# A graph network's node pipeline: bias and the second norm's h added to the convolution in its PSUM bank, x2 added from there, and no SBUF tile for x2 + h

## The chip, the core and the metric

The kernel runs on one core of a Trainium2 chip. The metric is the time of one execution on the device in microseconds, the median of several runs. The engines are named as in the profile: PE is TensorE (PEld its weight loads), DVE is VectorE, ACT is ScalarE, POOL is GpSimd, SP is SyncE.

## The reference

Four residual graph layers run over 100,000 nodes with 64 features and 25,000 edges. Most nodes are the end of no edge. For such a node a layer needs nothing but its own row:

```python
h = jnp.maximum(_layernorm(x, axis=-1), 0.0)
x = x + _L1_gnn_ref(h, src, dst, L1_gnn_fc_w, L1_gnn_fc_b)      # own row: x + h
h = jnp.maximum(_layernorm(x, axis=-1), 0.0)
x = x + _L2_gnn_ref(h, edge_index, L2_gnn_W1, L2_gnn_b1, L2_gnn_W2, L2_gnn_b2)
h = jnp.maximum(_layernorm(x, axis=-1), 0.0)
x = x + _L3_gnn_ref(h, edge_index, L3_gnn_W1, L3_gnn_b1, L3_gnn_W2, L3_gnn_b2)
```

The third layer (L2 in the names) gives `relu(h W1 + b1) W2 + b2 + h` for such a node. The row that goes into the last norm is therefore `x3 = x2 + h2 + conv + b2`, where x2 is the row before the layer, h2 its norm's output and conv the product of the second convolution. The change is in this sum.

## The kernel before

The first 560 us sort and prepare the edges. Then the main phase does two jobs at once, on the same engines, in one hand-written order:

- **Edges.** Six stages A to F, of 25 groups each. A group is 512 columns: its source rows are gathered (POOL, `mn_ring`, stages B to F), transposed, summed by a scan along the edges (`mn_total`, L1581), multiplied (`mn_scaled`, L1597), put through a weight product (L1933) and transposed back. Between two stages all rows must be in DRAM before POOL may gather them. Stage A gathers nothing; POOL meanwhile looks up 168 index tiles (`found`), which `late()` needs at the end of stage A (L1686).
- **Nodes.** 123 units of 1,024 nodes (25 of them, the "local" ones, are edge rows in stage A's order), each in a tile of 128 by 512. A unit passes through a pipeline of eight ticks; at tick t the units t to t - 7 are each at another step. The lists `TICKS_OF` say which ticks run in which group: about one in each group of A, C, E and F, two in three groups of B and D.

The steps of a tick that the change and the prediction touch, for the unit u = t - 3 where nothing else is said:

- PE, `first`, `second`, `third`: `conv1(2)` (L1206, bank 5), then further products, the edge group's `product` (L1933, it waits for `mn_scaled`), `variance(3)` (L1201), `conv2(2)` (L1211, bank 5), the transpose of x_in of unit t - 1 (bank 0), `conv2(3)` (L1211, bank 1). Then `center(3)` (L1197) reads x3 into bank 3; it waits for x3, and for `normalise(3)` of the unit before, which empties bank 3.
- ACT, `rest`: copies bank 0 to x2 of unit t - 1 (L1378); squares bank 3 (L1326); then, for units whose first norm is computed here, `row_deviation` (L1335, L1338), which stands behind those squares in ACT's order.
- DVE, `tail`: `normalise(2)` for unit t - 2 (h2, L1407), `node_res` = x2 + h2 for the same unit (L1425), x3 of unit t - 3 (L1431), `normalise(3)` for unit t - 4 (h3, L1407), and for unit t - 5 the pair y (L1442, in bank 1) and x4 (L1447). Then `h1` (L1452), which waits for ACT's `row_deviation`, and after it the edge group's scan.

Each engine takes its instructions strictly in this order; semaphores alone tie the engines together. Bank 5 holds conv1, then conv2 of one unit; PE may write the next unit's conv1 into it when x3 has been read out of it.

Of the kernel before, what the change touches and what calls it, by code (L numbers as in the profile page):

```python
# [11 lines left out]
ACT = mybir.ActivationFunctionType  # L12
# [1093 lines left out]
class Nodes:  # L1106
# [6 lines left out]
    def __init__(self, K, ctx):  # L1113
        def sb(name, r, shape=W):
            return ctx.enter_context(K["nc"].sbuf_tensor(f"node_{name}", [P, r, shape], F32))

        self.x_in, self.x2, self.res, self.x3 = sb("x_in", 3), sb("x2", 2), sb("res", 2), sb("x3", 3)
        self.h1, self.cent = sb("h1", 1), sb("cent", 1)
        self.h = {2: sb("h2", 2), 3: sb("h3", 2)}
        self.act = {2: sb("act2", 1), 3: sb("act3", 1)}  # L1120
        self.y, self.x4, self.rows = sb("y", 1), sb("x4", 2), sb("rows", 4)
        self.square, self.std = sb("square", 3), sb("std", 2)
        self.mean, self.var, self.lnv, self.rstd = (sb(a, 1, 8) for a in ("mean", "var", "lnv", "rstd"))
        self.s = sems(K["nc"], ctx, "node", "loaded:3 turned x2 res x3 y x4 outT out_rows stored:4 centered:n "
                      "squared:n var:n std:n rstd:n h:n conv1:n act:n conv2:n local_t:4 local_rows:4 mean1 cent1 x2_rows")
# [54 lines left out]
def node_tensor(K, nd, pe):  # L1180
    s, n, C, bank = nd.s, UNITS, K["C"], K["bank"]
# [96 lines left out]
    def third(t):  # L1278
        if 0 <= t - 3 < n:
            center(3, nd.x3[:, (t - 3) % 3, :], s["x3"], t - 3)  # L1280
        if local(t - 3):
            pe.wait_ge(s["x2"], t)
            turn(nd.act[2][:, 0, :], s["local_t"][2])
        if 0 <= t - 1 < n:
            center(2, nd.x2[:, (t - 1) % 2, :], s["x2"], t - 1)
        if local(t - 5):
            if local(t - 3):
                pe.wait_ge(s["local_rows"][2], t - 2)
            else:
                pe.wait_ge(s["x2"], t)  # L1290
            pe.wait_ge(s["act"][3], t - 4)
            turn(nd.act[3][:, 0, :], s["local_t"][3])
# [3 lines left out]
def node_scalar(K, nd, act):  # L1296
    s, n, C, bank = nd.s, UNITS, K["C"], K["bank"]

    def local(u):
        return 0 <= u < LOCALS  # L1300

    def log_var(i, u):
        act.wait_ge(s["var"][i], u + 1)
        need(act, s["h"][i], u)
        act.activation(nd.std[:, i - 2, :], bank[4][:, :], ACT.Ln, bias=C["eps"][:, 0:1]) \  # L1305
            .then_inc(s["std"][i], 1)

    def deviation(i, u):
        act.wait_ge(s["std"][i], u + 1)
        act.activation(nd.std[:, i - 2, :], nd.std[:, i - 2, :], ACT.Exp, scale=-0.5).then_inc(s["rstd"][i], 1)  # L1310

    def relu(i, u):
        act.wait_ge(s["conv1"][i], u + 1)
        if local(u - 1):
            act.wait_ge(s["local_t"][i], u)
        if u > 0 and i == 2:
            act.wait_ge(s["conv2"][2], u)
        elif u > LOCALS:
            act.wait_ge(s["conv2"][3], u - LOCALS)
        act.activation(nd.act[i][:, 0, :], bank[5 if i == 2 else 1][:, :], ACT.Relu, bias=C["bias"][:, 2 * i - 4:2 * i - 3]) \  # L1320
            .then_inc(s["act"][i], 1)

    def squares(i, u):
        act.wait_ge(s["centered"][i], u + 1)
        need(act, s["var"][i], u)
        act.activation(nd.square[:, i - 1, :], bank[i][:, :], ACT.Square).then_inc(s["squared"][i], 1)  # L1326

    def row_squares(u):
        act.wait_ge(s["cent1"], norms_until(u) + 1)
        act.activation(nd.square[:, 0, :], nd.cent[:, 0, :], ACT.Square).then_inc(s["squared"][1], 1)  # L1330

    def row_deviation(u):
        i = norms_until(u)
        act.wait_ge(s["var"][1], i + 1)
        act.activation(nd.lnv[:, 0, :], nd.var[:, 0, :], ACT.Ln, bias=C["eps"][:, 0:1], scale=1.0 / F) \  # L1335
            .then_inc(s["std"][1], 1)
        act.wait_ge(s["std"][1], i + 1)
        act.activation(nd.rstd[:, 0, :], nd.lnv[:, 0, :], ACT.Exp, scale=-0.5).then_inc(s["rstd"][1], 1)  # L1338

    def local_copy(kind, u):  # L1340
        act.wait_ge(s["local_t"][kind], u + 1)
        need(act, s["stored"][kind], u * 16)
        act.activation(nd.rows[:, kind, :], bank[0][:, :], ACT.Copy).then_inc(s["local_rows"][kind], 1)

    def begin(t):
        if 0 <= t - 3 < n:
            relu(2, t - 3)
        if 0 <= t - 2 < n:
            log_var(2, t - 2)

    def rest(t, between=None):
        if local(t - 3):
            local_copy(0, t - 3)
        if 0 <= t - 2 < n:
            deviation(2, t - 2)
        if LOCALS <= t - 6 < n:
            i = t - 6 - LOCALS
            act.wait_ge(s["outT"], i + 1)
            act.wait_ge(s["stored"][i % 4], 16 * (LOCALS + i // 4))
            act.activation(nd.rows[:, i % 4, :], bank[0][:, :], ACT.Copy).then_inc(s["out_rows"], 1)  # L1360
        if between:
            between()
        if 0 <= t - 5 < n:
            relu(3, t - 5)
        if 0 <= t - 4 < n:
            log_var(3, t - 4)
        if local(t - 5):
            local_copy(1, t - 5)
        if 0 <= t - 4 < n:
            deviation(3, t - 4)  # L1370
        if own_norm(t):
            row_squares(t)
        if 0 <= t - 1 < n:
            u = t - 1
            act.wait_ge(s["turned"], u + 1)
            need(act, s["centered"][2], u - 1)
            need(act, s["res"], u - 1)
            act.activation(nd.x2[:, u % 2, :], bank[0][:, :], ACT.Copy).then_inc(s["x2"], 1)  # L1378
        if 0 <= t - 3 < n:
            squares(3, t - 3)  # L1380
        if own_norm(t):
            row_deviation(t)
        if local(t - 3):
            local_copy(2, t - 3)
        if 0 <= t - 1 < n:
            squares(2, t - 1)
        if local(t - 5):
            local_copy(3, t - 5)
    return begin, rest


def node_vector(K, nd, v):
# [25 lines left out]

    def tail(t):
        if 0 <= t - 2 < n:  # L1420
            u = t - 2
            h = normalise(2, u)
            v.wait_ge(s["h"][2], u + 1)
            v.wait_ge(s["x2"], u + 1)
            v.tensor_tensor(nd.res[:, u % 2, :], nd.x2[:, u % 2, :], h, ALU.add).then_inc(s["res"], 1)  # L1425
        if 0 <= t - 3 < n:
            u = t - 3
            v.wait_ge(s["conv2"][2], u + 1)
            v.wait_ge(s["res"], u + 1)
            need(v, s["centered"][3], u - 2)  # L1430
            v.scalar_tensor_tensor(nd.x3[:, u % 3, :], bank[5][:, :], C["bias"][:, 1:2], nd.res[:, u % 2, :],  # L1431
                                   ALU.add, ALU.add).then_inc(s["x3"], 1)
        if 0 <= t - 4 < n:
            normalise(3, t - 4)
        if own_norm(t):
            v.wait_ge(s["squared"][1], norms_until(t) + 1)
            v.tensor_reduce(nd.var[:, 0, :], rows3(nd.square[:, 0, :]), AX.X, ALU.add).then_inc(s["var"][1], 1)
        if LOCALS <= t - 5 < n:
            u, i = t - 5, t - 5 - LOCALS
            v.wait_ge(s["conv2"][3], i + 1)  # L1440
            v.wait_ge(s["h"][3], u + 1)
            v.scalar_tensor_tensor(bank[1][:, :], bank[1][:, :], C["bias"][:, 3:4], nd.h[3][:, u % 2, :],  # L1442
                                   ALU.add, ALU.add).then_inc(s["y"], 1)
            v.wait_ge(s["y"], i + 1)
            v.wait_ge(s["x3"], u + 1)
            need(v, s["outT"], i - 1)
            v.scalar_tensor_tensor(nd.x4[:, u % 2, :], bank[1][:, :], 0.0, nd.x3[:, u % 3, :],  # L1447
                                   ALU.max, ALU.add).then_inc(s["x4"], 1)
        if own_norm(t):
            i = norms_until(t)  # L1450
            v.wait_ge(s["rstd"][1], i + 1)
            v.scalar_tensor_tensor(rows3(nd.h1[:, 0, :]), rows3(nd.cent[:, 0, :]), 0.0, wide(nd.rstd),  # L1452
                                   ALU.max, ALU.mult).then_inc(s["h"][1], 1)
            v.wait_ge(s["h"][1], i + 1)
            v.tensor_tensor(nd.x_in[:, t % 3, :], nd.x_in[:, t % 3, :], nd.h1[:, 0, :], ALU.add) \
                .then_inc(s["x2_rows"], 1)
# [628 lines left out]
```

## Time and profile before

| | |
|---|---|
| median of 3 runs | 2442.53 us (2442.11 to 2446.15) |
| span of the profiled execution | 2443.7 us |
| DVE, PE, POOL, ACT busy | 1845.2, 1785.7, 1781.6, 1377.4 us |
| stages A to F | A about 580 to 810 us, B to 1104, C to 1370, D to 1654, E to 1920, F to 2180, then POOL alone scatters the edge rows |

The profiled execution's own time is not given apart from its span, which lies 1.2 us above the median of the runs. A busy share over the whole span mixes the stages: what a change is worth is read from one tick of each stage.

### The profile page before, as it was taken

What the parts mean: (1) busy time and instruction counts of PE and PEld (TensorE: products, weight loads), DVE (VectorE), ACT (ScalarE), POOL (GpSimd) and SP (SyncE); (2) the same over time, 40 slices, a digit from 0 to 9 for tenths busy, and PEclk for the clock granted to TensorE, in tenths of its full rate; (3) what the DMA queues carried; (4) which work ended last, traced back from release to release, by engine and by line L of the source; (5) the groups of instructions that cost most, each with busy time, mean ns of one, the idle gap of its engine ahead of it and who ended that gap; (6) DMA issues with size and microseconds to landing.
All of it is one profiled execution on the core that took longest, in us unless ns stands there. A gap on an engine that the chain in (4) does not pass through costs nothing.

```text
span 2443.7 us, 26381 instructions
## 1 busy us (share of the span) xinstructions
PE 1785.7 (73%) x6414; PEld 872.1 (36%) x6414; DVE 1845.2 (76%) x3016; ACT 1377.4 (56%) x3086; POOL 1781.6 (73%) x1776
## 2 busy tenths in 40 slices
PE   3888888874998588878999878868999788860000
PEld 1333333322444244334444334434444344430000
DVE  6999998746888488986999688886999799960000
ACT  2766676632887365546888655546888666620000
POOL 6777777776777777736777577756777577777776
PEclk9999999986999799978999888988999899975555
DMA  3344443224776354434444356654444455440000
GB/s 71 90 124 129 127 123 97 71 75 132 233 240 216 115 182 128 133 115 107 129 131 130 102 167 188 184 170 115 128 130 129 112 139 136 129 133 22 23 21 20
DMA packets 223229, 302.24 MB, mean 124 GB/s; under 512 B 78896, under 2 KB 85165, under 8 KB 222952
## 3 DMA queue, kind: packets, MB, share of 16 engines
q1 hardware_dynamic: 166632, 249.64, 31.3%
q0 software_dynamic: 56448, 50.92, 11.6%
q8 instruction: 56, 0.92, 0.2%
q14 instruction: 93, 0.76, 0.1%
HBM read 156.13 MB, written 144.91 MB: 123 GB/s over the span
## 4 chain that ended last, share of the span: by engine, by line
DVE 23%; POOL 21%; issue 14%; PE 10%; ACT 6%; DMA 1%; DVEq 0%; POOLq 0%; SPq 0%; ACTq 0%
POOL mn_ring L529 13%; POOL out_dram L1889 8%; DVE node_h L1407 5%; PE bank L1197 5%; DVE mn_total L1581 4%; DVE node_x L1431 2%; DVE node_h L1452 1%; DVE mn_ring L1566 1%; ACT node_square L1326 1%; DVE node_mean L1414 1%; DVE mn_scaled L1597 1%; ACT node_std L1310 1%; PE bank L1206 1%; PE bank L1201 1%; PE bank L1191 1%
## 5 line engine op out<-in xcount | busy, mean ns | idle before, releaser
L529 POOL DMA_INDIRECT mn_ring<-slot_rows,addr_i x980 | 976.8, 997 | 390.4 <-issue 295.5
L1197 PE MATMUL bank<-node_x,center 128*128 128x512 f32 x492 | 250.8, 624 | 97.0 <-DVE node_h L1407 92.7
L1326 ACT ACTIVATE node_square<-bank 128x512 f32<-128x512 f32 x246 | 145.9, 593 | 222.6 <-PE bank L1197 222.6
L1201 PE MATMUL bank<-node_square,mean 128*128 128x512 f32 x492 | 265.5, 622 | 3.4 <-ACT node_std L1305 2.7
L1206 PE MATMUL bank<-node_h,wconv 128*128 128x512 f32 x492 | 266.1, 624 | 0.3 <-DVE mn_sums L1719 0.3
L529 POOL DMA_INDIRECT found<-node_table,look_i x196 | 209.7, 1070 | 74.9 <-issue 62.8
L529 POOL DMA_INDIRECT xin<-in_x_dram,src_i x192 | 195.2, 1017 | 64.3 <-issue 57.6
L529 POOL DMA_INDIRECT xin<-in_x_dram,dst_i x192 | 196.5, 1023 | 58.5 <-issue 58.5
L1889 POOL DMA_INDIRECT out_dram<-keep,scat_i x196 | 193.1, 985 | 62.5 <-issue 62.5
L1211 PE MATMUL bank<-node_act,wconv 128*128 128x512 f32 x442 | 230.9, 605 | 1.9 <-ACT node_act L1320 1.9
L1320 ACT ACTIVATE node_act<-bank,bias 128x512 f32<-128x512 f32 x246 | 170.5, 693 | 86.0 <-PE bank L1206 86.0
L1407 DVE SCALAR_TENSOR_TENSOR node_h<-bank,node_std 128x512 f32<-128x512 f32 x246 | 168.6, 686 | 54.0 <-ACT node_std L1310 52.2
L1305 ACT ACTIVATE node_std<-bank,eps 128x512 f32<-128x512 f32 x246 | 172.2, 700 | 23.1 <-PE bank L1201 22.6
L1581 DVE TENSOR_TENSOR_SCAN mn_total<-same,mn_total,bank 128x512 f32<-128x512 uint8 x120 | 150.2, 1251 | 25.6 <-PE bank L1918 25.4
L719 PE MATMUL bank<-fr_s_lo,fr_s_hi 128*128 128x392 f16 x392 | 138.5, 353 | 28.2 <-ACT fr_d_h L800 18.8
L1197 PEld LDWEIGHTS bank<-node_x,center 128*128 128x128 f32 x492 | 83.2, 194 | 211.6 <-DVE node_x L1431 152.2
L1310 ACT ACTIVATE node_std<-node_std 128x512 f32<-128x512 f32 x246 | 154.8, 629 | 5.3
L1201 PEld LDWEIGHTS bank<-node_square,mean 128*128 128x128 f32 x492 | 95.9, 199 | 136.3 <-issue 121.4
L800 ACT ACTIVATE fr_d_h<-fr_d_far,w 128x128 f16<-128x128 f16 x392 | 135.9, 394 | 6.4
L721 PE MATMUL bank<-fr_d_lo,fr_d_h 128*128 128x392 f16 x392 | 137.3, 350 | 0.0
L723 PE MATMUL bank<-fr_d_lo,fr_d_h 128*128 128x392 f16 x392 | 136.7, 349 | 0.0
L1933 PE MATMUL bank<-mn_scaled,wconv 128*128 128x512 f32 (+1 forms) x200 | 113.6, 652 | 28.9 <-DVE mn_scaled L1597 28.9
(337 smaller groups left out, 3807.0 us busy)
## 6 DMA issues: line engine op xcount, KB each, us to landing
out_dram<-node_rows SPq DMA_DIRECT2D x98, 256.0 KB, 3.4
mn_rin<-res SPq DMA_DIRECT2D x96, 256.0 KB, 3.6
slot_rows<-node_rows SPq DMA_DIRECT2D x96, 256.0 KB, 2.1
slot_rows<-keep SPq DMA_DIRECT2D x96, 256.0 KB, 2.3
mn_fcol<-f_rows SPq DMA_DIRECT2D x192, 128.0 KB
res<-mn_x SPq DMA_DIRECT2D x72, 256.0 KB, 3.0
node_x_in<-in_x_dram SPq DMA_DIRECT2D x64, 256.0 KB, 3.0
mn_ring<-slot_rows,addr_i POOLq DMA_INDIRECT x980
```

Source lines behind the costliest of these rows:

```text
L529: return eng.indirect_dma_start(out=dest, out_offset=None, in_=table, in_offset=bass.IndirectOffsetOnAxis(ap=index, axis=0))
L1197: pe.matmul(bank[i][:, :], C["center"][:, :], src, start=True, stop=True).then_inc(s["centered"][i], 1)
L1201: pe.matmul(bank[4][:, :], C["mean"][:, :], nd.square[:, i - 1, :], start=True, stop=True) \
L1206: pe.matmul(bank[5 if i == 2 else 1][:, :], C["wconv"][:, 2 * i - 4, :], nd.h[i][:, u % 2, :], start=True, stop=True) \
L1211: pe.matmul(bank[5 if i == 2 else 1][:, :], C["wconv"][:, 2 * i - 3, :], nd.act[i][:, 0, :], start=True, stop=True) \
L1305: act.activation(nd.std[:, i - 2, :], bank[4][:, :], ACT.Ln, bias=C["eps"][:, 0:1]) \
L1310: act.activation(nd.std[:, i - 2, :], nd.std[:, i - 2, :], ACT.Exp, scale=-0.5).then_inc(s["rstd"][i], 1)
L1320: act.activation(nd.act[i][:, 0, :], bank[5 if i == 2 else 1][:, :], ACT.Relu, bias=C["bias"][:, 2 * i - 4:2 * i - 3]) \
L1326: act.activation(nd.square[:, i - 1, :], bank[i][:, :], ACT.Square).then_inc(s["squared"][i], 1)
L1407: v.scalar_tensor_tensor(h, bank[i][:, :], 0.0, nd.std[:, i - 2, :], ALU.max, ALU.mult).then_inc(s["h"][i], 1)
L1581: v.tensor_tensor_scan(total[:, i % 2, 0:w], of_group(C["same"], g), source, 0.0 if g == 0 else total[:, 1 - i % 2, W - 1:W], ALU.mult, AL ...
L1889: gp.indirect_dma_start(out=K["out"], out_offset=bass.IndirectOffsetOnAxis(ap=C["scat"][:, t:t + 1], axis=0), in_=keep[:, t * F:t * F + F] ...
```

## The change

The sum x2 + h2 in SBUF is not computed. DVE adds bias and h2 of unit t - 3 to bank 5 in place, and then x2 from there to x3. h2 and x2 are thus read one tick later than before; x2 gets a third buffer for it, h2 keeps two. The semaphore `res` now counts the addition in the bank.

```diff
-        self.x_in, self.x2, self.res, self.x3 = sb("x_in", 3), sb("x2", 2), sb("res", 2), sb("x3", 3)
+        self.x_in, self.x2, self.x3 = sb("x_in", 3), sb("x2", 3), sb("x3", 3)
...
-            center(2, nd.x2[:, (t - 1) % 2, :], s["x2"], t - 1)
+            center(2, nd.x2[:, (t - 1) % 3, :], s["x2"], t - 1)
...
             need(act, s["centered"][2], u - 1)
-            need(act, s["res"], u - 1)
-            act.activation(nd.x2[:, u % 2, :], bank[0][:, :], ACT.Copy).then_inc(s["x2"], 1)
+            need(act, s["x3"], u - 2)
+            act.activation(nd.x2[:, u % 3, :], bank[0][:, :], ACT.Copy).then_inc(s["x2"], 1)
...
         if 0 <= t - 2 < n:
-            u = t - 2
-            h = normalise(2, u)
-            v.wait_ge(s["h"][2], u + 1)
-            v.wait_ge(s["x2"], u + 1)
-            v.tensor_tensor(nd.res[:, u % 2, :], nd.x2[:, u % 2, :], h, ALU.add).then_inc(s["res"], 1)
+            normalise(2, t - 2)
         if 0 <= t - 3 < n:
             u = t - 3
             v.wait_ge(s["conv2"][2], u + 1)
+            v.wait_ge(s["h"][2], u + 1)
+            v.scalar_tensor_tensor(bank[5][:, :], bank[5][:, :], C["bias"][:, 1:2], nd.h[2][:, u % 2, :],
+                                   ALU.add, ALU.add).then_inc(s["res"], 1)
             v.wait_ge(s["res"], u + 1)
+            v.wait_ge(s["x2"], u + 1)
             need(v, s["centered"][3], u - 2)
-            v.scalar_tensor_tensor(nd.x3[:, u % 3, :], bank[5][:, :], C["bias"][:, 1:2], nd.res[:, u % 2, :],
-                                   ALU.add, ALU.add).then_inc(s["x3"], 1)
+            v.tensor_tensor(nd.x3[:, u % 3, :], bank[5][:, :], nd.x2[:, u % 3, :], ALU.add).then_inc(s["x3"], 1)
```

What stands in DVE's order, in one tick of stage C, before. The names behind "waits" are those of the semaphores' numbers, some of them given to an earlier phase's name: `fr_h1T` counts conv2(2), `fr_squared` h2, `fr_xd_in0` x2, `fr_xd_in1` res, `ix_stored` center(3).

```order
1807 L1407 SCALAR_TENSOR_TENSOR node_h2<-bank2,node_std 128x512 [waits fr_rstd,fr_edges1]
1808 L1425 TENSOR_TENSOR node_res<-node_x2,node_h2 128x512 [waits fr_xd_in0,fr_squared]
1809 L1431 SCALAR_TENSOR_TENSOR node_x3<-bank5,bias,node_res 128x512 [waits ix_stored,fr_xd_in1,fr_h1T]
1810 L1407 SCALAR_TENSOR_TENSOR node_h3<-bank3,node_std 128x512 [waits fr_factor,fr_mean]
1811 L1437 TENSOR_REDUCE node_var<-node_square 128x8 [waits ix_spread]
```

And the same place in the changed kernel:

```order
1806 L1407 SCALAR_TENSOR_TENSOR node_h2<-bank2,node_std 128x512 [waits fr_rstd,fr_edges1]
1807 L1426 SCALAR_TENSOR_TENSOR bank5<-bank5,bias,node_h2 128x512 [waits fr_squared,fr_h1T]
1808 L1431 TENSOR_TENSOR node_x3<-bank5,node_x2 128x512 [waits ix_stored,fr_xd_in0,fr_xd_in1]
1809 L1407 SCALAR_TENSOR_TENSOR node_h3<-bank3,node_std 128x512 [waits fr_factor,fr_mean]
1810 L1436 TENSOR_REDUCE node_var<-node_square 128x8 [waits ix_spread]
```

The number of instructions is the same. The wait for conv2(2) stood before the second instruction behind h2, and now stands before the first. PE's order and ACT's order are unchanged.

## Rows read from the trace of the kernel before

**Rows 1.** The page: span, busy times, chain that ended last.

```profile
span 2443.7 us, 26381 instructions
...
PE 1785.7 (73%) x6414; PEld 872.1 (36%) x6414; DVE 1845.2 (76%) x3016; ACT 1377.4 (56%) x3086; POOL 1781.6 (73%) x1776
...
DVE 23%; POOL 21%; issue 14%; PE 10%; ACT 6%; DMA 1%; DVEq 0%; POOLq 0%; SPq 0%; ACTq 0%
```

**Rows 2.** Windows of stages C and F: length, busy times, PEclk, DMA share, GB/s.

```profile
1145.00:1350.00 205.00, 195.68 (x687) 97.88 (x685) 194.14 (x282) 178.66 (x443) 155.91 (x162) 1.00 0.49 129
...
1948.00:2120.00 172.00, 145.14 (x501) 71.93 (x502) 163.15 (x239) 111.10 (x209) 130.16 (x132) 1.00 0.50 137
```

**Rows 3.** Windows of x3 (L1431) alone, first to last start: length, busy.

```profile
1145.30:1349.25 203.95, 14.91 (x21) 1.00 0.49 129
1694.74:1899.25 204.51, 14.92 (x21) 1.00 0.48 129
622.28:779.79 157.51, 11.91 (x17) 1.00 0.75 240
```

**Rows 4.** Chain of waits, stage C: start, length, what.

```profile
1177.52 1.11 PE bank L1197 x2
...
1178.65 0.60 ACT node_square L1326
...
1179.47 0.22 ACT node_rstd L1338
```

**Rows 5.** Timeline of DVE, one tick of stage C: start, length, instruction.

```profile
1172.17 0.69 DVE L1597 TENSOR_TENSOR mn_scaled<-mn_total,mn_fcol 128x512 f32<-128x512 f32 x1
...
1174.70 0.68 DVE L1407 SCALAR_TENSOR_TENSOR node_h<-bank,node_std 128x512 f32<-128x512 f32 x1
1175.42 0.69 DVE L1425 TENSOR_TENSOR node_res<-node_x,node_h 128x512 f32<-128x512 f32 x1
1176.03 0.74 DVE L1431 SCALAR_TENSOR_TENSOR node_x<-bank,bias,node_res 128x512 f32<-128x512 f32 x1
1176.69 0.68 DVE L1407 SCALAR_TENSOR_TENSOR node_h<-bank,node_std 128x512 f32<-128x512 f32 x1
...
1177.88 0.75 DVE L1442 SCALAR_TENSOR_TENSOR bank<-bank,bias,node_h 128x512 f32<-128x512 f32 x1
1178.67 0.69 DVE L1447 SCALAR_TENSOR_TENSOR node_x<-bank,node_x 128x512 f32<-128x512 f32 x1
1179.71 0.69 DVE L1452 SCALAR_TENSOR_TENSOR node_h<-node_cent,node_rstd 128x512 f32<-128x512 f32 x1 [0.35 <-ACT node_rstd L1338]
```

**Rows 6.** Timeline of PE, the same tick of stage C.

```profile
1173.02 1.02 PE L1933 MATMUL bank<-mn_scaled,wconv 128*128 128x512 f32 x2
...
1174.73 1.02 PE L1211 MATMUL bank<-node_act,wconv 128*128 128x512 f32 x2
...
1177.52 1.96 PE L1197 MATMUL bank<-node_x,center 128*128 128x512 f32 x4 [0.47 <-DVE node_h L1407]
```

**Rows 7.** Timelines of DVE and PE, one tick of stage A.

```profile
642.79 0.69 DVE L1407 SCALAR_TENSOR_TENSOR node_h<-bank,node_std 128x512 f32<-128x512 f32 x1
```

```profile
643.63 1.10 PE L1197 MATMUL bank<-node_x,center 128*128 128x512 f32 x2 [0.25 <-DVE node_h L1407]
...
650.71 1.02 PE L1211 MATMUL bank<-node_act,wconv 128*128 128x512 f32 x2
```

**Rows 8.** Timeline of all engines, one tick of stage F.

```profile
1966.62 0.68 DVE L1641 TENSOR_TENSOR mn_part<-bank,mn_aux 128x512 f32<-128x512 f32 x1
...
1968.58 1.02 PE L1211 MATMUL bank<-node_act,wconv 128*128 128x512 f32 x2
...
1969.87 0.68 DVE L1407 SCALAR_TENSOR_TENSOR node_h<-bank,node_std 128x512 f32<-128x512 f32 x1
```

**Rows 9.** Waits over the span: who for whom, total us, times, longest.

```profile
POOL mn_ring L529 <- DMA slot_rows<-keep: 90.0, 4, 36.3
...
DVE mn_val L1686 <- DMA found<-node_table,look_i: 7.1, 2, 6.3
DVE node_x L1431 <- PE bank L1211: 5.1, 12, 1.2
```

## The prediction

> **What bounds the kernel now.** I read the page first. DVE is busy 76% of the span, PE and POOL 73% each, and the chain that ended last is shared by DVE (23%) and POOL (21%) [rows 1]. No engine bounds the whole, so I went on to single ticks, and of those to the three starts that the change touches: h2, conv2(2) and x3.
>
> In steady stage C, 20 ticks take 203.95 us from the first x3 to the last, 10.20 us a tick [rows 3]. The chain of waits in one of them runs from the h3 behind x3 to `center(3)` (1177.52), to ACT's squares of it (1178.65), to `node_rstd` (1179.47) and to h1 on DVE [rows 4]. DVE has been idle 0.35 us when h1 starts at 1179.71 [rows 5]. The rest of the loop is DVE's own order from h1 over the scan to the next h3. `center(3)` waited 0.47 us, and for h3, not for x3 [rows 6]. So in this stage whatever delays h3 delays `center(3)`, the squares, `node_rstd`, h1, the scan and the whole next tick. The 0.35 us is no cushion for h3: h1 starts at a fixed distance behind it (1176.69 to 1179.71, 3.02 us), through PE and ACT.
>
> POOL gathers beside this. At the four stage ends from B to F it waited 90.0 us in total, up to 36.3, for the rows of the stage before to be stored [rows 9]. A longer C or E thus moves the next stage's start by its whole length.
>
> **The change part by part.** It takes out `node_res` (0.69 us) and x3 with the bias (0.74), and puts in an addition in the bank and an addition of x2. The nearest rows for the new pair are y and x4, which do the same in bank 1: 0.75 and 0.69 [rows 5]. In busy time that is 1.43 against 1.44, nothing. What counts is start to start, and which start waits.
>
> Before, from h2: 0.72 to `node_res`, which waits for h2; 0.61 to x3, which waits for nothing of its own tick on DVE; 0.66 to h3 [rows 5]. That is 1.99. After, the first addition needs no result of this tick, so 0.61 (as from `node_res` to x3); then 0.79 to the addition of x2, which needs the first (as from y to x4, 1177.88 to 1178.67); then 0.61 to h3 (as behind `node_res`). That is 2.01: 0.02 us more. Wherever conv2(2) is early, the change costs about nothing. The one wait on h2 that goes is paid back by the one between the new pair.
>
> But conv2(2) is not early in stage C. It starts at 1174.73 and takes 1.02 [rows 6], so it ends at 1175.75. Before, it was first needed for x3 at 1176.03, which hid it. Now it is needed 0.61 behind h2, at 1175.31. With 0.04 for the semaphore (ACT started its squares 0.02 behind `center(3)`'s end, 1178.63 to 1178.65 [rows 4], and I take twice that) the first addition starts at 1175.79, the second at 1176.58, h3 at 1177.19 instead of 1176.69. **That is 0.50 us per tick.** Nothing gives it back. conv2(2) stands on PE two products behind the product of the edges (1173.02), which waits for `mn_scaled` (1172.17), and that hangs on the scan and on h1 [rows 5, 6]. The loop is closed: `mn_scaled`, product, conv2(2), the two additions, h3, `center(3)`, squares, `node_rstd`, h1, scan. It has no slack left, so each tick becomes 10.70 us. x2's third buffer costs nothing: ACT's copy waits for x3 of unit t - 4, made a tick ago.
>
> - **Stage C**: 20 ticks by 0.50 is 10.0. The tick before them (x3 at 1145.30) is one of 12 in which x3 already waited for conv2(2) [rows 9]. Such a tick pays what lies behind conv2(2): 0.79 + 0.61 - 0.66 = 0.74. Together 10.7.
> - **Stage E**: the same loop. Its 20 ticks take 204.51 [rows 3], 0.5 more than C's, waits for POOL's gathers that a slower DVE no longer meets. 20 by 10.70 is 214.0, so 9.5 more, and 0.7 for the tick before: 10.2.
> - **Stage A**: 17 x3 in 157.51 us, 9.84 a tick [rows 3]. Here `center(3)` starts at 643.63, 0.84 behind h3 (642.79), and conv2(2) ends at 650.71 + 1.02 = 651.73, PE working without a gap between [rows 7]. After the change h3 comes at 651.73 + 0.04 + 0.79 + 0.61 = 653.17, the next `center(3)` at 654.01: 10.38 a tick, 0.54 more, 9.2 over 17 ticks. But at the end of stage A DVE waits 7.1 us for POOL's last lookups [rows 9]. That cover takes 7.1; 2.1 is left.
> - **Two ticks behind the lookups**, before stage B: DVE does nothing but them there, one may be priced like C's steady tick, 0.50, the other as one that waited already, 0.74. Less what the first hides from the second, 1.1.
> - **Stage F**: conv2(2) ends at 1968.58 + 1.02 = 1969.60, and h2 starts only at 1969.87 [rows 8]. It is 0.9 early. F has another product's place and two more DVE steps per group. Nothing per tick; 0.7 for the one tick in which two stand behind each other, 0.2 for the last. 0.9.
> - **Stages B and D**: conv2(2) ends before the point needed in every steady tick, and D goes at POOL's pace. The ticks at the stage ends that pay 0.7 each lie beside POOL's first gathers, for which DVE waits longer. 0.
>
> Sum: 10.7 + 10.2 + 2.1 + 1.1 + 0.9 = 25.0 us. The profiled execution would go from 2443.7 to 2468.7; on the median that is 2442.5 + 25.0 = 2467.5 us.
>
> **The unknown costs, from both sides.** The step from the first addition to the second is read from y to x4, 0.79. At its least it is what a step costs without a result to wait for, 0.61; then a tick of C, E and A pays 0.32 and the sum is 20 x 2 x 0.32 + 1.4 in C and E, A hidden, 1 elsewhere: 15. At its most I take 0.1 more than y to x4: 0.60 a tick, 24 + 1.4 + 4 + 2 = 31, 2474. The nearest row is y to x4, the same engine, shape and memory, so I take it.
>
> Reading PSUM: an addition of two tiles takes 0.68 out of bank 7 (L1641, [rows 8]) and 0.69 out of SBUF (L1425, [rows 5]), no difference. The Trainium skill ("Perfetto Trace Analysis", Optimizing Scalar/DVE Operations) gives DVE a higher fixed cost per instruction on PSUM than on SBUF, about 125 ns against 60. By it the one more instruction on PSUM would add some 0.065 us a tick, an estimate of about 3 us over the ticks of C and E; the rows don't bear it out.
>
> A result to wait for: 0.72 behind h2, 0.61 where there is none [rows 5]. The Trainium skill ("VectorE: DVE Perf Modes", The DRAIN you can't avoid) says that chaining DVE instructions without semaphores between them wins nothing. By that rule the second step would not be dearer than an independent one, an estimate of 15 us for the whole; the two distances in the rows speak against it.
>
> **The rivals.**
> - *DVE's idle time takes it* (7%). If h1's wait were on something that does not hang on h3, the 0.35 us before h1 would hide most of 0.50, and 0.15 a tick were left in C and E: 6 + 3, 2451. Against it: the chain runs through `center(3)` and its squares [rows 4].
> - *Stage A's slowdown is not hidden* (6%), if POOL's lookups slow down with DVE. They wait for DVE's x of groups long done. It would add 7.1: 2475.
> - *The short step* (12%): 0.61 between the two additions, 15 us, 2458.
> - *Faster* (3%): conv2(2) comes 0.5 earlier than in the rows of C and E, since the DVE steps ahead of it move. Then only the lost wait on h2 would show, 0.11 a tick over the some 54 steady ticks of C, E and F, if the new pair's own wait were free: 6 us, 2436.6. It decides only if `mn_scaled` to conv2(2)'s end (3.58 us) shrinks below 3.1, and PE works through that time without a gap.
> - *PE's clock falls*, for PE now idles 0.5 more a tick. In F PE is busy 145.14 of 172 us, and the granted clock is 1.00, the 2.4 GHz level; in C it is 195.68 of 205, and would be about 91% after [rows 2]. So no, 2%.
>
> **How the numbers follow.** The forecast (70%) is 2467 us, its own range 2462 to 2472. With the short step and the upper bound of the costs, the range is 2458 to 2474. What can be told from no change is 0.2%, 4.9 us: slower than 2447.4 are all but the faster rival and part of the first. Slower 0.94, same 0.03, faster 0.03.
>
> **What the profile after would show.** The first addition waits for conv2(2) in every tick of A, C and E, 0.45 to 0.5 us in C and E; x3 is 10.7 us apart in C and E, 10.4 in A, unchanged in F. h1 still waits 0.35 us for `node_rstd`. DVE's busy time is within 3 us of 1845. The wait of L1686 for the lookups goes from 7.1 to nothing. The stages C and E are 10 us longer each, B, D and F are not. I am wrong if C's tick stays at 10.2, or if the wait for conv2(2) stands there and h1's wait shrinks by as much.

## The result, and the profile after

The changed kernel takes 2474.07 us (2472.73 to 2475.62, 4 runs), the kernel before on the same chip 2442.44 us (2442.11 to 2446.15, 4 runs). The ratio is 1.0118, 95% interval 1.0106 to 1.013: slower by 31.6 us. The forecast was 2467, its range 2458 to 2474: the measured time lies at the upper edge, 0.07 above it. The sign and the wait were right. In the profiled execution 30.1 us were lost where the sum has 25.0; around the end of stage A it was 8.8 us more than forecast, of which C and E gave some back.

The page of the changed kernel, its span and busy times. The profiled execution took 2475.62 us; its span is 30.1 us longer than that of [rows 1].

```profile
span 2473.8 us, 26381 instructions
...
PE 1775.8 (72%) x6414; PEld 866.4 (35%) x6414; DVE 1848.6 (75%) x3016; ACT 1377.3 (56%) x3086; POOL 1779.6 (72%) x1776
```

DVE is busy 3.4 us longer, the others are busy for less. So nearly all of the 30 us is idle time, and the page can't say where it is.

The windows of x3 (L1431) alone, first to last start, stages A, C and E, as in [rows 3]: length, DVE busy, PEclk, DMA share, GB/s.

```profile
621.13:786.99 165.86, 11.06 (x16) 1.00 0.71 228
1155.01:1369.19 214.18, 13.83 (x20) 1.00 0.47 124
1713.97:1928.16 214.19, 13.84 (x21) 1.00 0.47 125
```

In A there are 17 x3 in both kernels, thus 16 ticks from first to last (the changed kernel's last x3 starts just behind the window's end, so its row counts 16). Over the same 16, 20 and 20 ticks these are 8.35, 10.23 and 9.68 us longer: 0.52, 0.51 and 0.48 us a tick. Where it goes shows on DVE's timeline of one tick of stage C (start, length, instruction, idle time before it and who ended it; against [rows 5]):

```profile
1195.95 0.69 DVE L1407 SCALAR_TENSOR_TENSOR node_h<-bank,node_std 128x512 f32<-128x512 f32 x1
1197.04 0.76 DVE L1426 SCALAR_TENSOR_TENSOR bank<-bank,bias,node_h 128x512 f32<-128x512 f32 x1 [0.41 <-PE bank L1211]
1197.84 0.69 DVE L1431 TENSOR_TENSOR node_x<-bank,node_x 128x512 f32<-128x512 f32 x1
1198.44 0.68 DVE L1407 SCALAR_TENSOR_TENSOR node_h<-bank,node_std 128x512 f32<-128x512 f32 x1
...
1201.46 0.69 DVE L1451 SCALAR_TENSOR_TENSOR node_h<-node_cent,node_rstd 128x512 f32<-128x512 f32 x1 [0.35 <-ACT node_rstd L1338]
```

The first addition (L1426) waits 0.41 us for PE. The second follows 0.80 behind it and h3 0.60 behind that. h1 still waits 0.35 for `node_rstd`: the idle time in front of h1 has taken up nothing, as [rows 4] had said.

PE's timeline in the same tick:

```profile
1194.23 1.05 PE L1932 MATMUL bank<-mn_scaled,wconv 128*128 128x512 f32 x2
...
1195.98 1.02 PE L1211 MATMUL bank<-node_act,wconv 128*128 128x512 f32 x2
```

conv2(2) ends at 1197.00 and the addition starts at 1197.04. conv2(2) stands 1.75 us behind the product, 1.71 in [rows 6].

In stage F the first addition doesn't wait (DVE's timeline, against the h2 of [rows 8]):

```profile
1999.93 0.68 DVE L1407 SCALAR_TENSOR_TENSOR node_h<-bank,node_std 128x512 f32<-128x512 f32 x1
2000.53 0.75 DVE L1426 SCALAR_TENSOR_TENSOR bank<-bank,bias,node_h 128x512 f32<-128x512 f32 x1
2001.31 0.69 DVE L1431 TENSOR_TENSOR node_x<-bank,node_x 128x512 f32<-128x512 f32 x1
2001.92 0.68 DVE L1407 SCALAR_TENSOR_TENSOR node_h<-bank,node_std 128x512 f32<-128x512 f32 x1
```

The waits over the span (who for whom, total us, times, longest), DVE's and then POOL's, against [rows 9]:

```profile
DVE bank L1426 <- PE bank L1211: 43.6, 75, 1.5
...
DVE mn_val L1685 <- DMA found<-node_table,look_i: 7.2, 2, 6.3
```

```profile
POOL mn_ring L529 <- DMA slot_rows<-keep: 119.8, 4, 41.3
```

The wait for conv2(2) went from 5.1 us in 12 ticks to 43.6 in 75. POOL's wait for the rows of the stage before went from 90.0 to 119.8, 29.8 more: a later stage end makes POOL wait. (The two figures near 30 are not one account: by the pages POOL's lookups took 8.1 us more too, and its gathers 9.1 less.) And one line is not as forecast: DVE's wait for the lookups, which should have gone from 7.1 us to nothing, is still 7.2.

Where the 30.1 us were lost, from the starts of DVE's scans in both traces. The scan of one group is taken in each, and the changed kernel's start less that of before is the delay. The changed kernel's execution came to stage A 1.0 us early, so what stage A cost is one more than its delay:

| up to | delay, us | lost in this stretch | forecast |
|---|---|---|---|
| A, group 0 | -1.0 | -1.0 | 0 |
| A, group 24 | 7.0 | 8.0 | 9.2, less 7.1 of cover |
| POOL's last lookup | 7.1 | | 2.1 |
| B, group 2 | 12.0 | 4.9 | 1.1 |
| B, group 24 | 11.9 | 0 | 0 |
| C, group 3 | 10.0 | -1.9 | |
| C, group 24 | 20.8 | 10.8 | 10.7 with the row above |
| D, group 24 | 21.1 | 0.2 | 0 |
| E, group 3 | 19.5 | -1.5 | |
| E, group 24 | 29.3 | 9.8 | 10.2 with the row above |
| end | 30.1 | 0.8 | 0.9 |

**The lookups.** POOL's last lookup starts at 811.92 before and at 818.99 after. It issues them one behind the other, 0.30 us apart, and has no instruction that the change touches. Its timeline in one tick of stage A, of the kernel before, with the one instruction of DVE during which the first of these lookups starts:

```profile
641.35 0.69 DVE L1425 TENSOR_TENSOR node_res<-node_x,node_h 128x512 f32<-128x512 f32 x1
641.56 1.30 POOL L529 DMA_INDIRECT found<-node_table,look_i  x1 [0.30 <-issue]
643.17 0.94 POOL L529 DMA_INDIRECT found<-node_table,look_i  x1 [0.30 <-issue]
...
648.43 1.42 POOL L529 DMA_INDIRECT found<-node_table,look_i  x1 [0.30 <-issue]
...
651.40 1.30 POOL L529 DMA_INDIRECT found<-node_table,look_i  x1 [0.30 <-issue]
```

and of the changed kernel, with one instruction of DVE too:

```profile
684.66 1.90 POOL L529 DMA_INDIRECT found<-node_table,look_i  x1 [0.30 <-issue]
686.87 0.94 POOL L529 DMA_INDIRECT found<-node_table,look_i  x1 [0.30 <-issue]
...
689.48 0.68 DVE L1657 SCALAR_TENSOR_TENSOR mn_h<-mn_cent,mn_rstd 128x512 f32<-128x512 f32 x1
689.56 1.42 POOL L529 DMA_INDIRECT found<-node_table,look_i  x1 [0.30 <-issue]
...
695.03 1.90 POOL L529 DMA_INDIRECT found<-node_table,look_i  x1 [0.30 <-issue]
```

From 641.56 to 651.40 there are 7 lookups and 9.84 us, DVE's tick; from 684.66 to 695.03 again 7, and 10.37 us, DVE's new tick. 14 lookups further the pattern repeats to 0.01 us in both (19.69 and 20.73 us apart). The longer tick doesn't hold more lookups, it holds longer ones: 1092 ns on average before, 1159 after. The one of 1.90 us starts 0.13 us into a scan of DVE:

```profile
684.53 1.28 DVE L1580 TENSOR_TENSOR_SCAN mn_total<-same,mn_total,mn_ring 128x512 f32<-128x512 uint8 x1
```

The scan has 1.15 us left, and the lookup takes 0.96 more than a free one. In the kernel before no lookup of the steady ticks starts so early in a scan: they start with at most 0.26 us of it left and are held by at most 0.08. So far that is a picture and no cause.

### The profile page after: what moved, and what is told of

Its sections match the earlier page's. It is cut to its first block, busy times and chain, and to the rows that moved or that the text cites. A ratio compares the mean times of both kernels' runs of the same rounds, so it can differ in the third digit from the quotient of the medians.

```text
span 2473.8 us, 26381 instructions
## 1 busy us (share of the span) xinstructions
PE 1775.8 (72%) x6414; PEld 866.4 (35%) x6414; DVE 1848.6 (75%) x3016; ACT 1377.3 (56%) x3086; POOL 1779.6 (72%) x1776
## 4 chain that ended last, share of the span: by engine, by line
PE 27%; POOL 17%; DVE 17%; issue 11%; ACT 3%; DMA 1%; DVEq 0%; POOLq 0%; SPq 0%; ACTq 0%
POOL mn_ring L529 9%; POOL out_dram L1888 8%; PE bank L1197 7%; PE bank L1201 5%; PE bank L1206 5%; DVE node_h L1407 4%; DVE bank L1426 3%; PE bank L1191 3%; PE bank L1211 2%; DVE mn_total L1580 2%; PE bank L1932 2%; PE bank L1917 1%; DVE mn_h L1657 1%; PE bank L1948 1%; DVE mn_cent L1603 1%
## 5 line engine op out<-in xcount | busy, mean ns | idle before, releaser
L529 POOL DMA_INDIRECT found<-node_table,look_i x196 | 217.8, 1111 | 74.9 <-issue 62.5
L1407 DVE SCALAR_TENSOR_TENSOR node_h<-bank,node_std 128x512 f32<-128x512 f32 x246 | 168.1, 683 | 55.6 <-ACT node_std L1310 55.4
```

The costliest lines, as they stand in the source:

```text
L529: return eng.indirect_dma_start(out=dest, out_offset=None, in_=table, in_offset=bass.IndirectOffsetOnAxis(ap=index, axis=0))
L1407: v.scalar_tensor_tensor(h, bank[i][:, :], 0.0, nd.std[:, i - 2, :], ALU.max, ALU.mult).then_inc(s["h"][i], 1)
```

## The experiments

The theories. **Theory 1** is the prediction's: the loss is the wait of the first addition for conv2(2), in A, C and E alone. **The rivals** are that reading x2 and h2 a tick later costs something, and that what is lost beside the wait comes from POOL: either its lookups wait for DVE's x, or DVE's instructions hold them up. Ratios are to the kernel before, run on the same chip between the runs of each experiment. That kernel took 2442.4, 2446.7, 2455.2 and 2445.0 us on the four chips, so absolute times of different groups are not compared.

### The third buffer alone

```diff
-        self.x_in, self.x2, self.res, self.x3 = sb("x_in", 3), sb("x2", 2), sb("res", 2), sb("x3", 3)
+        self.x_in, self.x2, self.res, self.x3 = sb("x_in", 3), sb("x2", 3), sb("res", 2), sb("x3", 3)
```

with x2's index modulo 3 where it is used. The copy into x2 still waits for `res`.

> The kernel before with x2 in three buffers and nothing else changed; x2 + h2 is still summed in SBUF for unit t - 2. Theory 1 (the change's cost is the wait for conv2(2) in front of the first addition): same as before, 2442 us within 2. Rival (the third buffer's other addresses or the changed wait of the copy cost something): 3 us or more slower.

2446.20 against 2446.74 us, ratio 1.000 (0.999 to 1.001). The buffer costs nothing.

### The sum in SBUF, a tick later

With x2 in three buffers, and the copy into it waiting for `res` of one unit earlier:

```diff
         if 0 <= t - 2 < n:
-            u = t - 2
-            h = normalise(2, u)
+            normalise(2, t - 2)
+        if 0 <= t - 3 < n:
+            u = t - 3
             v.wait_ge(s["h"][2], u + 1)
             v.wait_ge(s["x2"], u + 1)
-            v.tensor_tensor(nd.res[:, u % 2, :], nd.x2[:, u % 2, :], h, ALU.add).then_inc(s["res"], 1)
+            v.tensor_tensor(nd.res[:, u % 2, :], nd.x2[:, u % 3, :], nd.h[2][:, u % 2, :], ALU.add).then_inc(s["res"], 1)
```

> The kernel before, with x2 + h2 summed in SBUF for unit t - 3 instead of t - 2, between h2 and x3, and x2 in three buffers. h2 and x2 are read as late as in the changed kernel, but conv2(2) is waited for in front of x3 alone, the second instruction behind h2. Start to start it is 0.61 to the sum, 0.72 to x3, as before. Theory 1 (the wait for conv2(2) ahead of the first addition): 2442 us within 3, ticks of 10.2 in stage C. Rival (reading h2 and x2 a tick later is what costs): near the changed kernel, 2465 or more.

2451.27 us (2448.35 to 2458.80), ratio 1.0023 (1.0012 to 1.0033): 4.5 us slower where no change was expected. Reading x2 and h2 a tick later is thus not what the change pays for, 4.5 of some 30 us at most. Where the 4.5 us come from is not shown. Its profiled execution is the longest of its ten (2458.80); in it a tick of C and E is 10.25 us instead of 10.19, some 2 us over 40 ticks. But 10.24 also stands in stage C of the kernel with the changed form in A alone, whose C has the form before, and 10.18 in its E. So such a tick comes without the later read too.

### The sum ahead of h2

The same two blocks in the other order, x2 in three buffers as there: first `node_res` of unit t - 3, then h2 of unit t - 2, then x3. On DVE nothing waits for the instruction ahead of it, and conv2(2) is needed as late as before.

> As the run with the sum a tick later, but the sum of x2 and h2 for unit t - 3 stands ahead of h2 of unit t - 2. Nothing in the row sum, h2, x3 then needs the instruction in front of it: h2 to x3 is 0.61 instead of 1.33, sum to x3 1.22. x3 of stage C is due 0.11 us earlier than before, 0.13 behind conv2(2)'s end. Theory 1: 0.11 a tick less in C and E (4.4 us) and F (1.5), something in B, nothing or little in A, where conv2(2) comes just in time: 2433 to 2439 us. Rival (the loop of a tick is closed through something else): 2442.

2437.49 us, ratio 0.9969 (0.9958 to 0.998). It was run again on another chip.

> The run with the sum first once more, beside the next one on the same chip. 0.996 to 0.998 of before.

2435.77 us, ratio 0.9965 (0.9952 to 0.9978). It beats both kernels, by 0.3%. But stages C and E were not shortened: a steady tick of C takes 10.18 us, against 10.19 before, where 0.11 less was expected. DVE's timeline of stage C, in the first of the two runs:

```profile
1175.85 0.68 DVE L1424 TENSOR_TENSOR node_res<-node_x,node_h 128x512 f32<-128x512 f32 x1
1176.45 0.68 DVE L1407 SCALAR_TENSOR_TENSOR node_h<-bank,node_std 128x512 f32<-128x512 f32 x1
1177.05 0.74 DVE L1432 SCALAR_TENSOR_TENSOR node_x<-bank,bias,node_res 128x512 f32<-128x512 f32 x1
1177.80 0.69 DVE L1407 SCALAR_TENSOR_TENSOR node_h<-bank,node_std 128x512 f32<-128x512 f32 x1
```

`node_res` to x3 takes 1.20 us instead of 1.33 [rows 5, h2 to x3], and h3 follows 0.75 behind x3, not 0.66: it now comes when ACT has its `node_std` ready. The gain is in the other stages. In the second run's trace, 1.0 us less lie between the scans of B's groups 2 and 24, 2.1 between C's last scan and D's, and 4.2 between E's last and F's; a steady tick of F takes 11.38 us instead of 11.57.

### The same, with variance(3) ahead of the product

PE's `variance(3)` is put ahead of the edges' product, and ACT's deviation for h3 with it, so that `node_std` comes earlier.

```diff
+        if 0 <= t - 4 < n:
+            need(pe, s["std"][2], min(t - 1, n))
+            need(pe, s["std"][3], t - 4)
+            variance(3, t - 4)
         if between:
             between()
-        if 0 <= t - 4 < n:
-            need(pe, s["std"][2], min(t - 1, n))
-            need(pe, s["std"][3], t - 4)
-            variance(3, t - 4)
```

> The run with the sum first, in whose stage C x3 came 0.11 us earlier but h3 did not: it waited for ACT's node_std. Here, in stages C, E and F, variance(3) stands ahead of the edges' product on PE, and ACT's copy of that product stands behind both node_std steps of unit t - 4. node_std comes some 0.7 us earlier, the product 0.86 later. Theory (the tick of C and E is closed through h3, whatever feeds it): h3 follows x3 by 0.66 instead of 0.75, a tick of C and E is 10.09 instead of 10.19, 4 us less than the sum first: 0.994 to 0.996 of before. Rival (the later product closes the tick, since the group's transposes back wait for it): same as the sum first, or slower.

2436.96 us, ratio 0.997 (0.9962 to 0.9979): nothing gained on the version above, as the rival has it; what closes the tick is conv2(2), which stands behind the later product. DVE's timeline of stage C:

```profile
1181.12 0.68 DVE L1407 SCALAR_TENSOR_TENSOR node_h<-bank,node_std 128x512 f32<-128x512 f32 x1
1181.85 0.75 DVE L1432 SCALAR_TENSOR_TENSOR node_x<-bank,bias,node_res 128x512 f32<-128x512 f32 x1
```

h3 is no longer late, but x3 comes 0.73 behind h2 and not 0.60: it now waits for conv2(2), which ends at 1181.81. One wait of 0.1 us was exchanged for another. In stage C of these versions the way over PE (conv2(2)) and the way over ACT (`node_std`) stand within some 0.1 us of DVE's own order. That fits with the changed kernel's wait of 0.41 us being paid in full.

### The changed kernel, conv2(2) earlier on PE

In the changed kernel conv2(2) is put ahead of `variance(3)`, one product earlier.

```diff
+        if 0 <= t - 3 < n:
+            conv2(2, t - 3)
         if 0 <= t - 4 < n:
             need(pe, s["std"][2], min(t - 1, n))
             need(pe, s["std"][3], t - 4)
             variance(3, t - 4)
...
-        if 0 <= t - 3 < n:
-            conv2(2, t - 3)
```

> The changed kernel with conv2(2) ahead of variance(3) on PE, 0.86 us earlier; variance(3) comes 0.86 later. In stage C conv2(2) then ends before the first addition is due, so that wait goes. But variance(3) feeds node_std and h3: its end moves to where conv2(2)'s was, and ACT needs 1.3 us more for Ln and Exp, so h3 starts no earlier than 1.4 behind that point, which is where it starts now. Theory 1 extended (the loop closes through PE's order, whichever of the two is last): 2470 to 2478, the wait on DVE moves from the first addition to h3. Rival (only the first addition's wait counts): back to 2450 or less.

2484.55 against 2455.22 us, ratio 1.0114 (1.0097 to 1.0131), as the changed kernel without it. The 2470 to 2478 expected on a before of 2442 are ratios of 1.011 to 1.015. DVE's timeline of stage C:

```profile
1204.65 0.75 DVE L1426 SCALAR_TENSOR_TENSOR bank<-bank,bias,node_h 128x512 f32<-128x512 f32 x1
1205.43 0.69 DVE L1431 TENSOR_TENSOR node_x<-bank,node_x 128x512 f32<-128x512 f32 x1
1206.52 0.69 DVE L1407 SCALAR_TENSOR_TENSOR node_h<-bank,node_std 128x512 f32<-128x512 f32 x1 [0.40 <-ACT node_std L1310]
```

The first addition no longer waits; h3 waits 0.40 instead, for the `node_std` that hangs on the delayed `variance(3)`, and the tick is 10.7 us, as in the changed kernel. This narrows theory 1: the wait for conv2(2) is where the loss shows, but h3 has a second way behind the edges' product, through `variance(3)` and ACT, that is as long once `variance(3)` stands behind conv2(2): h3 starts 2.47 us behind h2 here and 2.49 in the changed kernel. Exchanging the two products doesn't shorten the tick.

### The changed form in some stages only

Both forms of x3 in one kernel, chosen by the stage in which the unit's x3 falls:

```diff
+            if banked(u):
+                v.scalar_tensor_tensor(bank[5][:, :], bank[5][:, :], C["bias"][:, 1:2], nd.h[2][:, u % 2, :],
+                                       ALU.add, ALU.add).then_inc(s["banked"], 1)
...
+                v.tensor_tensor(nd.x3[:, u % 3, :], bank[5][:, :], nd.x2[:, u % 3, :], ALU.add).then_inc(s["x3"], 1)
+            else:
```

In B, D and F:

> The changed form only in the ticks of stages B, D and F, where conv2(2) ends before either form needs it; the form before in A, C and E. Theory 1: same as before within 2 us (ratio 0.999 to 1.001), ticks of stage F as long as before. Rival (the additions in the bank cost DVE time of their own, wherever they stand): 0.1 us or more for each of the some 59 units, ratio 1.002 or more.

2445.43 against 2444.99 us, ratio 0.9998 (0.9989 to 1.0007). In these three stages together the change costs nothing that this run can tell, about 2 us either way.

In C and E:

> The changed form (additions in bank 5) only for units whose x3 falls in a tick of the stages C and E; elsewhere the form before; x2 in three buffers. Theory 1 (0.50 to 0.52 us a tick of C and E for the wait for conv2(2)): 10 us in each of C and E less some 2 us given back at each stage's start, 2459 to 2463 where before is 2442 (ratio 1.007 to 1.009), and the lookups end as before. Rival (most of the loss is stage A's): ratio under 1.005.

2476.43 against 2455.22 us, ratio 1.0086 (1.0069 to 1.0103), as theory 1 has it. In its trace the ticks of C and E are 10.7 us.

In A:

> The changed form only in the ticks of stage A. If POOL's lookups really take the length of DVE's ticks, stage A's 0.52 us a tick over 17 ticks arrives at stage B: 9 to 12 us, ratio 1.004 to 1.005, lookups ended at about 819. By the step of the prediction (POOL's lookups go at their own pace and cover stage A): 2 to 3 us, ratio 1.001.

2463.03 against 2455.22 us, ratio 1.0035 (1.0023 to 1.0046). 0.86% and 0.35% add up to 1.21%, the whole change to 1.18%. So stage A costs some 8 us, where the sum had 3.2 with the two ticks behind the lookups. The ratio is a little under the 1.004 to 1.005 expected of a stage A that isn't hidden, and its interval leaves out the 1.001 of a hidden one.

Executions come to stage A at times up to 10 us apart, so the lookups are compared by their own length, from the start of the first of stage A's 168 to that of the last. It is 241.0 us before (570.87 to 811.92) and 249.2 after (569.75 to 818.99), 8.2 more. With the changed form in A alone it is 249.1. With it in C and E alone, on the same chip, it is 240.9, and in B, D and F alone 240.9.

### What paces the lookups

First, whether the lookups wait for DVE's x. Every eighth tests that semaphore. With this edit to the changed kernel none does:

```diff
-LOOK_PACE = 8
+LOOK_PACE = 1000
```

> The changed kernel, with POOL's lookups of stage A no longer waiting for DVE's x of the groups (the wait after every eighth is gone). In the changed kernel the lookups ended 7 us later than before, as DVE's stage A did. Theory A (POOL's instructions themselves take longer where they meet DVE's, seven of them in each DVE tick): same as the changed kernel, 2474 within 2, one lookup in eight still takes 1.9 us. Rival (the wait for DVE's x paces them): 5 to 7 us faster, 2467 to 2469.

2474.43 against 2446.74 us, ratio 1.0114 (1.01 to 1.0129), as the changed kernel. The lookups take 249.0 us from first to last. It is not the semaphore. Then, whether it takes the additions in the bank at all: the kernel before, with one more addition on DVE in stage A, whose result nobody reads.

```diff
+        if t < 24 and 0 <= t - 3:
+            need(v, s["spare"], t - 3)
+            v.wait_ge(s["x2"], t - 2)
+            v.tensor_tensor(nd.spare[:, 0, :], nd.h[2][:, (t - 3) % 2, :], nd.h[2][:, (t - 3) % 2, :], ALU.add).then_inc(s["spare"], 1)
```

> The kernel before with one more addition of a tile with itself on DVE (0.6 us, its output read by nobody) between x3 and h3, in the ticks of stage A alone; no change in the bank. It lengthens stage A's ticks without touching conv2(2) or bank 5. If the length of DVE's tick paces the lookups: they end 7 to 9 us later than before and the kernel is 9 to 13 us slower (ratio 1.004 to 1.005). If it was the additions in the bank that disturbed POOL: the lookups end as before, and the kernel is at most 3 us slower.

2463.25 against 2455.22 us, ratio 1.0042 (1.0027 to 1.0057). DVE's timeline of stage A, one tick:

```profile
685.33 0.74 DVE L1432 SCALAR_TENSOR_TENSOR node_x<-bank,bias,node_res 128x512 f32<-128x512 f32 x1
685.99 0.68 DVE L1437 TENSOR_TENSOR node_spare<-node_h 128x512 f32<-128x512 f32 x1
...
695.60 0.74 DVE L1432 SCALAR_TENSOR_TENSOR node_x<-bank,bias,node_res 128x512 f32<-128x512 f32 x1
```

The tick is 10.27 us, and 7 lookups take 10.27 us too (from the start at 692.22 to that at 702.49). From the first to the last they take 248.3 us, 7.3 more than before, with no addition in the bank anywhere. The groups of the lookups between 600 and 800 us (count, busy us, mean ns, idle time before), of the kernel before, the changed one, this one and the one without the semaphore:

```profile
L529 POOL DMA_INDIRECT found<-node_table,look_i x141 | 153.9, 1092 | 46.6 <-issue 46.6
```

```profile
L529 POOL DMA_INDIRECT found<-node_table,look_i x135 | 156.5, 1159 | 44.8 <-issue 44.8
```

```profile
L529 POOL DMA_INDIRECT found<-node_table,look_i x135 | 155.2, 1150 | 45.5 <-issue 45.5
```

```profile
L529 POOL DMA_INDIRECT found<-node_table,look_i x135 | 156.4, 1158 | 44.5 <-issue 44.5
```

All three with the longer tick have 135 lookups where before has 141. The pace of the lookups is that of DVE's ticks: shown. Over all runs of this document, the eight traces whose stage A has the tick of before (9.84 us) have 239.4 to 242.7 us from the first lookup to the last, the five with a longer one (10.27 to 10.37 us) 247.9 to 249.2. The spare addition reads SBUF twice, as `node_res` does, but it is not its own reads that slow the lookups: those that start in it take 0.96 us, 0.01 to 0.02 more than a free one. The profiled executions of this kernel and of the one with the changed form in A are the shortest of their runs (2450.6 and 2455.2 us), so their traces give the pace of stage A and not the medians.

## Why the prediction was 7 us short

- **The wait and the tick** ("That is 0.50 us per tick"): right. The steps forecast from h2 were 0.61 and a wait of 0.48, then 0.79 and 0.61; the trace has 1.09 from h2 to the first addition, 0.80 and 0.60. The loop is closed, h1's wait stayed at 0.35, and the tick is 0.51 us longer in C. The run with conv2(2) earlier adds what the prediction didn't have: taking this wait away is not enough, since `variance(3)` then comes too late by as much.
- **The step between the additions**: y to x4 was the right row. 0.80 measured, 0.79 taken, and the short step of 0.61 did not occur. The additions also show nothing dearer about PSUM: 0.76 and 0.69 us, against 0.75 and 0.69 for y and x4.
- **C 10.7 and E 10.2**: from group 3 to group 24 they lost 10.8 and 9.8. I missed that each stage starts 1.9 and 1.5 us less late than the one before ended; DVE's waits for gathers got shorter (35.6 us in all before, the longest 7.3; 22.1 and 5.0 after). Net 8.9 and 8.2. The changed form in C and E alone measured 0.86%.
- **B, D 0 and F 0.9**: 0, 0.2 and 0.8 in the trace, so right. The form in these three alone measured 0.9998, which can't tell 0.9 us from nothing.
- **The failed step is "That cover takes 7.1; 2.1 is left"**. The tick of stage A became 0.52 us longer where 0.54 was forecast, DVE came 7.0 us later to the end of the stage, and POOL's last lookup 7.1 us later too (8.0 and 8.1, counted from stage A's start). The wait between them stayed 7.2, and the cover hid nothing. I had read the lookups as work that doesn't depend on DVE, since the one semaphore they test was long past. Taking that semaphore away changed nothing, so the reading of the semaphore was right; the pace comes another way. This was the rival "stage A's slowdown is not hidden", to which I gave 6% and the price of 2475, 1 us from what was measured. That the time still lies at the edge of the range is luck: the upper bound of 2474 was worked out from a dearer step between the two additions, which did not occur.
- **Two ticks behind the lookups, 1.1**: mis-sized, 4.9 measured up to group 2 of stage B. Of these, 2.4 stand at group 0 (2.4 too with the changed form in A alone, 2.1 with the spare addition). But from the last lookup to that scan the unchanged stretch took 32.2 us in the profiled kernel before, 33.4 with the third buffer alone and 32.9 with the changed form in C and E, against 34.6 after; so 1.2 to 2.4 are left for the change.
- **The other 2.5** of the 4.9 lie between the scans of groups 0 and 2, 17.97 us after and 15.44 before, and are not the change's. There TensorE's granted clock falls in the changed kernel's trace. The same fall stands in the trace of the kernel with the third buffer alone (17.94 us), and it is missing in that of the changed kernel without the semaphore (15.46 us). The windows, in this order (length, busy times of PE, PEld, DVE, ACT, POOL, PEclk, DMA share, GB/s):

```profile
857.10:863.90 6.80, 6.08 (x17) 3.94 (x18) 4.53 (x6) 1.95 (x4) 5.28 (x6) 0.50 0.15 30
```

```profile
848.90:855.70 6.80, 6.02 (x18) 3.87 (x18) 4.54 (x6) 1.90 (x4) 5.28 (x6) 0.50 0.16 30
```

```profile
858.50:866.00 7.50, 6.72 (x24) 3.25 (x24) 5.22 (x7) 3.39 (x6) 5.67 (x7) 1.00 0.14 27
```

  The clock is 0.50, the 1.2 GHz level, in the first two and 1.00 in the third. In the 23.9 us at 1.00 ahead of its fall, PE was busy 18.5 us in the changed kernel; ahead of the third window it was busy 17.1 of 21.7, and the clock did not fall. What decides it stays open. In this pair of traces it adds 2.5 us to the loss; how often it falls in the executions behind the medians is not known.

Against the sum, the trace has -1.0 for the early start, +6.0 for the cover, +3.8 behind it (2.5 of them the clock's), -1.8 and -2.0 in C and E, and about 0 elsewhere: 5.1 us, from 25.0 to 30.1. The medians differ by 1.5 us more than the traces, which no trace places.

**Why POOL keeps DVE's time.** The rows show that 7 lookups fall in each tick, whether it lasts 9.84, 10.27 or 10.37 us. What grows is the time for which lookups are held, over the 0.94 us of a free one, and the steady ticks of stage A in all these traces show one pattern. A lookup that starts while DVE works on an instruction with two inputs in SBUF is held by what is left of that instruction, less 0.12 or 0.13 us (less 0.16 to 0.20 for the scan):

| lookup starts in | left of it, us | held, us |
|---|---|---|
| `node_res` (L1425, before) | 0.48 | 0.36 |
| the edges' `mn_ring` (L1557 before, L1556 after) | 0.32 | 0.20 |
| the edges' norm (L1658 before, L1657 after) | 0.60 | 0.48 |
| the spare addition | 0.14 | 0.01 |
| the scan, with the spare addition | 0.67 | 0.48 |
| the scan, after | 1.15 | 0.96 |
| a norm out of a bank (L1407, before) | 0.32 | 0 |
| the addition of x2 out of the bank (L1431, after) | 0.61 | 0 |
| the reduction of one tile (L1602, before) | 0.24 | 0 |

The holds of one tick add up to 1.1 us before, 1.5 with the spare addition and 1.6 after, and with 7 free lookups and their gaps (7 x 1.25) that is the tick each time, within 0.03 us. The Trainium skill ("SBUF — State Buffer", Who interferes with whom) says that a DVE instruction with two SBUF inputs contends with a GpSimd instruction that reads SBUF, and that the order of issue decides which of the two is blocked. The trace agrees for the lookups, 0.96 us held against 1.15 left of the scan. It does not show the other direction: DVE's instructions with two SBUF inputs that start during a lookup take 0.68 or 0.69 us and the scan 1.28, as elsewhere. So the statement at the start of this document that semaphores alone tie the engines together does not hold for POOL and DVE. What is worked out but not shown: 8 free lookups with their gaps take 8 x 1.25 = 10.0 us, more than the tick of 9.84, and of the longer ticks they leave only 0.27 or 0.37 us for being held, no more than one hold of the kind in `node_res` (0.36); and a lookup that is released towards the end of a DVE instruction starts its successor at a fixed distance from it, so the pattern locks to the tick. No run tried a tick long enough for 8.

**What beats both kernels** is the sum in SBUF taken a tick late and ahead of h2: 0.9969 and 0.9965. It gets rid of the wait between h2 and the sum without asking for conv2(2) any sooner. The change got rid of the same wait, and moved the wait for PE up by one instruction.

## What to carry to other kernels

Fusing an addition into the place where its operand arrives saves nothing in busy time if the number of instructions stays, but it moves the wait for that operand ahead of work that used to hide it: look at when the operand comes and when it is first needed, in each stage apart. Before idle time is counted as cover, ask whether the work that one waits for would keep its pace when one's own engine slows down; a semaphore that is long past doesn't prove it, the start distances of both engines over some ticks do. Where an execution's start moves by several us from one to the next, compare lengths within a trace and not times since its start, and compare the granted clock before a difference is given to the change. Where three engines stand within 0.1 us of each other in a loop, moving a product up on one of them only moves the wait.

## What the runs showed of the hardware

POOL's indirect lookups, with no semaphore between them and DVE that they had to wait for, ran in lockstep with DVE's ticks: 7 per tick in ticks of 9.84, 10.27 and 10.37 us, single ones of 0.94 us stretched up to 1.90. Each was held by what was left of the DVE instruction with two SBUF inputs in which it started, less 0.12 to 0.20 us, and by nothing in instructions that read a bank or one tile. TensorE's granted clock fell to 0.50 for 6.8 us at one place of stage B in some executions and not in others, with and without the change, and stretched the 15.4 us around it to 17.9. An addition into PSUM in place of SBUF costs nothing measurable in its own length (0.75 to 0.76 us in bank 5, 0.74 for x3 with the bias into SBUF), while the step to an instruction that needs the result was 0.80 against some 0.60 without such a need.
